# Three interleaved convolutional GRU scans: the new value's argument formed in the accumulator instead of on VectorE

## What is computed

```python
def step(h, xr):
    gi = x @ wih.T;  gh = h @ whh.T            # three gates each: r, z, n
    r = sigmoid(ir + hr);  z = sigmoid(iz + hz)
    n = tanh(i_n + r * h_n)
    out = (1 - z) * n + z * h                  # the step's context, kept
    h_new = tanh(conv1d(out, cw, cb))          # 3 taps along the line
    return h_new, out
```

## Time and profile before

| | before |
|---|---|
| median of three runs | 404.64 us |
| span of the profiled execution | 401.3 us |
| TensorE matmul busy | 360.2 us, 2702 matmuls |
| VectorE busy | 296.8 us, 750 instructions |
| ScalarE busy | 275.4 us, 573 instructions |
| scan, from block 5 on | about 59 to 322 us of the span |
| combining of the chunks k = 2 and after | 332.6 us to the end |

### The profile page before, as it was taken

How to read it: one execution, slowest core, us unless ns; L and a number is a source line. 1 busy time by engine, 2 the same in 40 slices (tenths; PEclk the granted TensorE clock), 3 DMA queues, 4 the chain that set the end, 5 groups by cost and what they waited for, 6 DMA issues and landing times.

```text
span 401.3 us, 7957 instructions
## 1 busy us (share of the span) xinstructions
PE 360.2 (90%) x2702; PEld 262.5 (65%) x2702; DVE 296.8 (74%) x750; ACT 275.4 (69%) x573; POOL 15.9 (4%) x26
## 2 busy tenths in 40 slices
PE   0105789999999999999999999999999999999996
PEld 0002668888888888888888888888888861222221
DVE  0659989899898898998998998998988982212111
ACT  6538878888878888888788788888888869000000
POOL 1074010000000000000000000000000000000000
PEclk9999999999999999999999999999999997689688
DMA  8700000000000000000000000000000001111112
GB/s 311 304 0 1 1 2 2 0 0 0 0 0 0 0 0 0 0 0 0 0 0 0 0 0 0 0 0 0 0 0 0 0 0 54 70 61 52 53 52 78
DMA packets 4183, 10.43 MB, mean 26 GB/s; under 512 B 593, under 2 KB 721, under 8 KB 4177
## 3 DMA queue, kind: packets, MB, share of 16 engines
q1 hardware_dynamic: 4176, 10.36, 6.7%
HBM read 6.16 MB, written 4.19 MB: 26 GB/s over the span
## 4 chain that ended last, share of the span: by engine, by line
PE 84%; ACT 6%; DVE 4%; issue 2%; POOL 2%; DMA 1%; SPq 0%; ACTq 0%; POOLq 0%
PE rz_bank L683 19%; PE conv_bank L683 15%; PE rz_bank L686 10%; PE n_bank L683 10%; PE conv_bank L686 7%; PE n_bank L686 5%; PE n_bank L776 3%; PE n_bank L774 3%; PE rz_bank L772 3%; PE n_bank L772 3%; PE rz_bank L776 3%; PE rz_bank L774 3%; DMA ctx_store<-weights_dram 1%; ACT rz L405 1%; ACT ctx_store L340 1%
## 5 line engine op out<-in xcount | busy, mean ns | idle before, releaser
L683 PE MATMUL conv_bank<-ctx_store,w_parts 128*128 (+1 forms) x558 | 108.9, 275 | 2.6 <-ACT ctx_store L428 2.1
L683 PE MATMUL rz_bank<-h_parts,w_parts 128*128 128x256 f16 x372 | 76.2, 273 | 0.1
L405 ACT ACTIVATE rz<-rz_bank,descale 128x512 f32<-128x512 f32 x96 | 66.0, 688 | 7.6 <-PE rz_bank L683 2.4
L686 PE MATMUL conv_bank<-ctx_store,w_parts 128*128 (+1 forms) x279 | 67.2, 275 | 0.0
L683 PEld LDWEIGHTS conv_bank<-ctx_store,w_parts 128*128 128x128 f16 x558 | 54.2, 97 | 19.1 <-ACT ctx_store L428 8.4
L417 ACT ACTIVATE nval<-npre 128x256 f32<-128x256 f32 x93 | 38.5, 414 | 40.5 <-DVE npre L625 40.5
L613 DVE SCALAR_TENSOR_TENSOR npre<-n_bank,descale,rz 128x256 f32<-128x256 f32 x93 | 45.0, 484 | 24.4 <-ACT rz L405 24.2
L683 PE MATMUL rz_bank<-x_rows,w_parts 128*128 (+1 forms) x256 | 52.4, 273 | 1.9 <-issue 1.9
L422 ACT ACTIVATE hval<-conv_bank,biases,descale 128x256 f32<-128x256 f32 x93 | 52.2, 561 | 0.0
L683 PE MATMUL n_bank<-h_parts,w_parts 128*128 128x256 f16 x186 | 45.7, 273 | 0.0
L686 PE MATMUL rz_bank<-h_parts,w_parts 128*128 128x256 f16 x186 | 45.6, 273 | 0.0
(11 more groups left out here) (89 smaller groups left out, 526.5 us busy)
## 6 DMA issues: line engine op xcount, KB each, us to landing
x<-x_dram SPq DMA_DIRECT2D x8, 512.0 KB, 9.1
out_dram<-x_rows SPq DMA_DIRECT2D x16, 256.0 KB, 2.0
ctx_store<-weights_dram SPq DMA_DIRECT2D x3, 576.0 KB, 5.0
ctx_store<-weights_dram SPq DMA_DIRECT2D x1, 192.0 KB, 6.0
biases<-biases_dram SPq DMA_DIRECT2D x1, 2.0 KB, 11.4
```

The lines of the kernel that those rows point to most:

```text
L405: nc.scalar.activation(rz[k][:].rearrange("p g c -> p (g c)"), rz_bank[k][:], ACT.Sigmoid, scale=gate_scale(k)).then_inc(sig_done[k], 1)
L683: last = nc.tensor.matmul(out, w_block(HI, k, n), parts(hi_or_lo), start=start, stop=stop and hi_or_lo == LO, skip_group_check=True)
L686: last = nc.tensor.matmul(out, w_block(LO, k, n), parts(HI), start=False, stop=False, skip_group_check=True)
```

## The change

The new value's recurrent product now goes to columns 0:256 of `n_bank[k]` (it starts the accumulation there). VectorE multiplies it by r in place, in the accumulator. Then TensorE adds the input product of n onto it, and the tanh reads the bank with the scale that the first step used before. VectorE's addition (line 625) and the buffer `npre` go. The three matmuls of n from x leave `input_products` at the end of a block. They become `new_products`, which run one pair later in the skew, between the HI and the LO part of a convolution, behind a wait for the multiplication. `z_times_h` waits for the multiplication. Two waits at the end of the scan change their semaphore.

```diff
             def new_value(k, s):
-                if is_first(s):
-                    act.wait_ge(n_ready[k], 1)
-                    nc.scalar.activation(nval[k][:], n_bank[k][:, 0:COLS], ACT.Tanh,
-                                         scale=gate_scale(k)).then_inc(n_done[k], 1)
-                else:
-                    act.wait_ge(npre_done[k], s)
-                    nc.scalar.activation(nval[k][:], npre[k][:], ACT.Tanh).then_inc(n_done[k], 1)
+                act.wait_ge(n_full[k], s + 1)
+                nc.scalar.activation(nval[k][:], n_bank[k][:, 0:COLS], ACT.Tanh,
+                                     scale=gate_scale(k)).then_inc(n_done[k], 1)
...
             def reset_hidden(k, s):
                 dve.wait_ge(sig_done[k], s + 1)
-                dve.wait_ge(n_ready[k], s + 1)
-                nc.vector.scalar_tensor_tensor(npre[k][:], n_bank[k][:, COLS:2 * COLS], gate_scale(k),
-                                               rz[k][:, 0, :], ALU.mult, ALU.mult).then_inc(rh_done[k], 1)
+                dve.wait_ge(n_ready[k], s)
+                nc.vector.tensor_tensor(out=n_bank[k][:, 0:COLS], in0=n_bank[k][:, 0:COLS],
+                                        in1=rz[k][:, 0, :], op=ALU.mult).then_inc(rh_done[k], 1)
...
-            def tanh_argument(k, s):
-                dve.wait_ge(rh_done[k], s)
-                nc.vector.scalar_tensor_tensor(npre[k][:], n_bank[k][:, 0:COLS], gate_scale(k),
-                                               npre[k][:], ALU.mult, ALU.add).then_inc(npre_done[k], 1)
...
-            def z_times_h(k):
+            def z_times_h(k, s):
+                dve.wait_ge(rh_done[k], s)
                 nc.vector.tensor_tensor(out=rz[k][:, 0, :], in0=rz[k][:, 1, :], in1=hval[k][:], op=ALU.mult)
...
             def input_products(k, s):
...
-                passes(n_bank[k][:, 0:COLS], k, 2, x_parts, HI, start=True)
-                last = passes(n_bank[k][:, 0:COLS], k, 2, x_parts, LO, stop=first)
-                if first:
-                    last.then_inc(n_ready[k], 1)
+            def new_products(k, s):
+                first = is_first(s)
...
+                ahead(pe, s, x_parts(HI), x_parts(LO))
+                if not first:
+                    pe.wait_ge(rh_done[k], s)
+                passes(n_bank[k][:, 0:COLS], k, 2, x_parts, HI, start=first)
+                passes(n_bank[k][:, 0:COLS], k, 2, x_parts, LO, stop=True).then_inc(n_full[k], 1)
 
             def hidden_products(k, s):
...
-                passes(n_bank[k][:, COLS:2 * COLS], k, GATES + 2, parts, HI)
-                passes(n_bank[k][:, COLS:2 * COLS], k, GATES + 2, parts, LO, stop=True) \
+                passes(n_bank[k][:, 0:COLS], k, GATES + 2, parts, HI, start=True)
+                passes(n_bank[k][:, 0:COLS], k, GATES + 2, parts, LO, stop=True) \
                     .then_inc(n_ready[k], 1)
 
-            def convolution(k, s):
+            def convolution(k, s, between):
...
                 for part in (HI, LO):
                     if part == LO:
+                        between()
                         pe.wait_ge(ctx_lo_done[k], s + 1)
...
             def steps(t, j):
+                def new_of_last():
+                    k, s = lagged(t, j, 1)
+                    if exists(s):
+                        new_products(k, s)
+
                 k, s = lagged(t, j, 2)
                 if exists(s, STEPS - 2):
-                    convolution(k, s)
+                    convolution(k, s, new_of_last)
+                else:
+                    new_of_last()
                 if j == 2 and isinstance(t, int) and t == STEPS - 1:
                     pe.wait_ge(w_lo_done, SETS)
-                    pe.wait_ge(npre_done[0], STEPS - 1)
+                    pe.wait_ge(n_done[0], STEPS)
...
-            pe.wait_ge(npre_done[1], STEPS - 1)
+            pe.wait_ge(n_done[1], STEPS)
```

More of the change, by code:

```diff
@@ L78, in build @@
         rz = [sb(f"rz_{k}", [C, 2, COLS], f32) for k in range(DIRS)]
-        npre = [sb(f"npre_{k}", [C, COLS], f32) for k in range(DIRS)]
         nval = [sb(f"nval_{k}", [C, COLS], f32) for k in range(DIRS)]
@@ L162, in build @@
         rh_done = per_dir("rh_done")
-        npre_done = per_dir("npre_done")
+        n_full = per_dir("n_full")
         n_done = per_dir("n_done")
@@ L650, in steps @@
                     context_lo(*now)
-                if exists(nxt[1]) and not is_first(nxt[1]):
-                    tanh_argument(*nxt)
                 if exists(before[1], STEPS - 2):
@@ L655, in steps @@
                 if exists(nxt[1]) and not is_first(nxt[1]):
-                    z_times_h(nxt[0])
+                    z_times_h(*nxt)
             dve.wait_ge(sides_zero, DIRS)
@@ L688, in passes, with x_line @@
                 return last
+            def x_line(k, s, part):
+                store = x_col if k == 2 else x_rows[:, :, line(k, s), :, :]
+                return store[:, part, :, :].rearrange("p b l -> p (b l)")
             def input_products(k, s):
@@ L693, in x_parts @@
                 def x_parts(part):
-                    store = x_col if k == 2 else x_rows[:, :, line(k, s), :, :]
-                    return store[:, part, :, :].rearrange("p b l -> p (b l)")
+                    return x_line(k, s, part)
                 ahead(pe, s, x_parts(HI), x_parts(LO))
@@ L708, in input_products, with x_parts @@
                     last.then_inc(rz_ready[k], 1)
[L709 to L714, removed]
-                passes(n_bank[k][:, 0:COLS], k, 2, x_parts, HI, start=True)
-                last = passes(n_bank[k][:, 0:COLS], k, 2, x_parts, LO, stop=first)
-                if first:
-                    last.then_inc(n_ready[k], 1)
+            def new_products(k, s):
+                first = is_first(s)
+                def x_parts(part):
+                    return x_line(k, s, part)
+                ahead(pe, s, x_parts(HI), x_parts(LO))
[3 more added lines that the diff above has]
+                passes(n_bank[k][:, 0:COLS], k, 2, x_parts, LO, stop=True).then_inc(n_full[k], 1)
             def hidden_products(k, s):
```

## The result

| | before | changed |
|---|---|---|
| median | 404.30 us (4 runs, 402.24 to 406.71) | 433.26 us (4 runs, 432.07 to 434.10) |
| ratio to before, 95% interval | | 1.0724 (1.0675 to 1.0773) |
| span of the profiled execution | 401.3 us | 430.9 us |
| time of that execution | | 432.64 us |
| TensorE matmuls, busy | 2702, 360.2 us | 2702, 375.7 us |

The kernel is 29 us slower. VectorE did lose its 93 additions and 37 us of busy time, and TensorE's matmuls are as many as before.

What follows compares the result with a forecast made beforehand. TensorE was full and the chain from last r and z matmul to next convolution (1.37 us) would outlast its queued matmuls, cut from 1.43 to 1.10; 22.9 + 1.6 + 1.6 = +26.1 us gave 430.7 us, range 422 to 440.

Steps and rivals of the forecast that it cites:

- The steady part: Scan's 88 blocks: each goes from 2.99 to 3.25 us because TensorE waits for `context_hi`; +22.9 us.
- The second rival, part of the stall hidden: Steady blocks take 3.10 to 3.20 us, matmuls closer after a wait or chain shorter: 417 to 426 us; chance 0.09.
- The first rival, TensorE's own work: Steady blocks stay at 27 matmuls, 2.97 us, if the chain is shorter than the cover left: 406.1 us; chance 0.05.
- VectorE's addition worth nothing: Steady blocks: removing VectorE's addition, 0.48 us a block, gains nothing by itself, being outside the chain.
- The multiplication at 0.48 us and hidden: VectorE's multiplication in the accumulator takes 0.48 us (bounds 0.42 and 0.75), under the 0.97 us available, so costs nothing.
- Register work: Address computation for new products on TensorE's queue between the convolution's parts: 0 us, at most 0.1 us a block.
- The clock: TensorE idle 0.27 of 3.25 us a block: clock stays 2.4 GHz; rival at 1.2 GHz gives above 600 us, chance 0.02.
- The start-up: Scan's first pairs: the tanh of n waits for new products queued behind a waiting convolution; +1.6 us, bounds 0 and 1.9.
- The last pairs: End of the scan: the last pair's new products stand ahead of 18 chunk matmuls; 10.17 becomes 11.8 us, +1.6 us.
- The span and the run: Profiled span goes from 401.3 to 427.4 us; the runs' median lies 3.3 us above the span.
- the combining: Stage after the scan: nothing in it changes, matmuls run at either clock level; 0 us, +-3.

Runs made afterwards that it cites:

- new_after_first_tap: Changed kernel with the new products behind the first tap of the convolution's HI part instead of behind all three taps: 430.70 us.
- before_cover_minus2: Kernel before without two of the three matmuls of n's input product in steps 1 to 31: 402.88 us.
- context_hi_on_vector: Changed kernel with `context_hi` moved from ScalarE to VectorE, straight behind the blend: 406.47 us.
- cover_plus2: Changed kernel with two more matmuls a block between the last r and z matmul and the next convolution: 432.20 us.
- multiplication_late: Changed kernel with two more VectorE products of 256 columns ahead of every multiplication in the accumulator: 450.29 us.

## Why the prediction was right

It forecast 430.7 us and a range of 422 to 440; 433.26 were measured. By its steps:

**The steady part: right.** It said 3.25 us a block and +22.9 us; 3.257 us and +23.5 were measured. Every link stood in the trace as summed: 1.88 us from the convolution to the last r and z matmul, 0.31 to the sigmoid, 0.59 to `context_hi` (0.58 forecast), 0.42, and 0.05. That the links are the cause, and not only add up, is shown by four runs: two matmuls in the cover cost 0.000 us a block, two in the loop 0.218, the sigmoid taken out of the chain gives 0.265 back, and fewer matmuls in the kernel before give 0.007.

**The second rival, part of the stall hidden: wrong.** It wanted 3.10 to 3.20 us a block.

**The first rival, TensorE's own work: wrong,** by the same runs. The Trainium skill, "Perfetto Trace Analysis", Identifying the Most-Contended Engine, says which engine to optimize first, the one with the highest occupancy; for TensorE it wants the share of the weight loads or of the peak in place of matmul busy time. It gives no time for a change. That an unchanged load means an unchanged time was the prediction's reading of it for this rival, and the measurement disagrees with that reading. By matmul busy time TensorE was the fullest engine in the steady part before and after (263.13 of 263.13 us, 276.44 of 286.60), and its number of matmuls stayed the same; what changed was how many of them stood between a signal and the instruction that needed its answer.

**VectorE's addition worth nothing: right.** With one operation put back the block is 3.256 us.

**The multiplication at 0.48 us and hidden: right, smaller.** It took 0.433 us on average (40.3 us for 93), between the bounds 0.42 and 0.75, and its wait never showed in the steady part. Register work for the new products left no trace either: they start 0.68 us behind the convolution, the distance of six matmuls.

**The tanh from the bank.** Not in the sum: it takes 474 ns with the bank as its source and a scale, 414 before from the buffer, 93 x 0.06 = 5.6 us more on ScalarE in all. It is off the chain, so it costs nothing.

**The clock: right for the steady part.** The granted clock is 1.00 there, 2.4 GHz, with TensorE busy 276.44 of 286.60 us; the new waits did not lower it. The Trainium skill, "TensorE: Matmul & The Clock Gate", Part 1, says that half rate is the default and that activity lifts it. The trace agrees in so far as the clock stayed up while TensorE had work in every block.

**The start-up: the mis-sized term.** Forecast +1.6 us, with bounds of 0 and 1.9; the stage grew by 3.4. It splits at the first convolution, 45.42 before and 47.97 after. From there to the fifth, both at full speed, it is 13.84 us before and 15.52 after, +1.7. By turns, with what was forecast, it is +1.36 (1.37), +0.33 (0.35), +0.04 (nothing) and -0.05 (-0.3): the first two are right, and the 0.3 us that VectorE's relief was to bring back in the fourth turn did not come. Ahead of the first convolution it is 3.77 us before and 5.52 after, +1.75 where 0.18 was forecast. In new_after_first_tap, whose first matmuls ran at full speed, that piece is 3.95 us (41.68 to 45.63), and 3.95 - 3.77 is just the 0.18. By that comparison the other 1.6 us come from the first matmuls of the scan, which ran at half speed. Before:

```profile
41.65:44.60 2.95, 2.95 (x27) 2.54 (x27) 2.92 (x6) 2.88 (x5) 0.00 (x0) 1.00 0.01 3
```

and in the changed kernel:

```profile
42.45:45.60 3.15, 3.15 (x15) 2.17 (x16) 2.36 (x3) 1.78 (x2) 0.00 (x0) 1.00 0.01 3
```

27 matmuls in 2.95 us, 15 in 3.15. The change isn't needed for it: of the 13 profiles of this case 10 begin so, among them three with the order of the kernel before (before_cover_minus2 and both runs with `context_hi` on VectorE). The profile of the kernel before is one of the three without. This is the step where one profiled execution was taken for the rule.

**The last pairs: right.** Forecast +1.6 us, 11.8 in all; measured +1.57, 11.74. The granted clock was 1.00 and the chunk matmuls kept their 0.23 us.

**The span and the run.** The prediction added 3.3 us for what lies around the span, the difference between the median and the one profiled span. In the changed kernel the profiled execution's own time is 432.64 for a span of 430.9, 1.7 us. The rest of the 3.3 was scatter between executions. That it lies in the combining is likely and not shown: in the profiles of both kernels only that stage has a granted clock under 1.00, and slower executions of the kernel before have a lower mean clock (407.01 us at 0.954, 402.63 us at 0.972). The span was forecast 3.5 us too short (427.4 against 430.9): start-up 1.8, the later first matmul 0.8, steady part 0.6, combining 0.3. The too large term around the span, 3.3 against 433.26 - 430.9 = 2.4, took 0.9 of it back, so that 430.7 stands against 433.26. That much of the closeness is luck; the 23 us of the steady part are not.

## What to carry to other kernels

An engine that is busy all the time can still have no slack in a wait: count what it has queued between giving a signal and needing the answer, and compare it with the chain of that answer, before moving anything out of that stretch. Work moved from cover to the other side costs its own time although the engine does no more of it, and relief of an engine that isn't in the chain (VectorE here) is worth nothing until something of the chain is given to it. Where two limits stand level, as 2.98 and 2.97 us a block here, taking work off either one alone gains little (0.007 and 0.023 us a block).

## What was not expected of the hardware

- At the start of the scan 256-column matmuls started 0.21 us apart in 10 of 13 profiles and 0.11 apart in the other three. 0.21 is the distance of the lower level: 512 columns take 0.23 and 0.43 us at the two. The view of windows prints a granted clock of 1.00 for both (the two windows above). For the slow one that is no measurement: where the trace has no entry of the clock, the view counts it as 1.00. The changed kernel's first entry stands at 45.68 us, and the distance falls from 0.21 to 0.11 between 45.40 and 45.76. In all ten profiles the distance of 0.21 ends within 0.3 us of the first entry (44.98 to 51.02 us); in the kernel before, the first entry is at 40.02, ahead of the scan. So a 1.00 ahead of the first entry says nothing, and the distance tells the speed.
- Where there is an entry, it and the distance agree. context_hi_on_vector began the scan at 0.11, fell to 0.21 from 43.2 us on and was back at 0.11 with the convolution at 46.61:

```profile
43.00:46.50 3.50, 3.14 (x17) 1.90 (x14) 2.64 (x7) 2.67 (x5) 0.00 (x0) 0.53 0.01 2
```

- What decides between the two speeds wasn't found out. The kernel before and cover_plus2 have the same work on TensorE ahead of the scan, to 0.01 us (eight matmuls of 512 columns from 36.19 and 36.20, then 1.89 us idle up to 41.65 and 41.66), and one went on at full speed and the other at half.
- A VectorE product with its source and its result in an accumulator bank took 433 ns, against 420 with all in SBUF; the multiplication before, with the bank as source and two multiplications, took 484. A tensor_scalar of 272 columns from float32 to float16 took 0.30 us, where the same on ScalarE took 0.42.
- VectorE operations in a row start about 0.34 us apart although each lasts 0.43 (219.47 and its followers in the changed kernel; in multiplication_late two of them last 0.76 together), so an operation put into its queue costs less there than its duration.
